# First conditioned norms, transposes and values of an attention block, for three of five tiles, made inside the block before it

## The reference, cut to what matters

```
# fourth layer: hidden = gelu(xn @ w1[e]); expert_out = hidden @ w2[e]; out = sum over e of gate * expert_out
x = x + L1_ffn(layernorm(x))
# fifth layer, on h = layernorm(x), four times:
y = ((h - mean) / sqrt(var + eps)) * (1 + scale) + bias     # scale = cond @ sw + sb, bias = cond @ bw + bb
q, k, v = y @ wq + bq, y @ wk + bk, y @ wv + bv             # 4 heads of 128
h = h + attention(q, k, v over the edges) @ wo + bo
y = (the same conditioned norm with second weights)
h = h + relu(y @ m_w1 + m_b1) @ m_w2 + m_b2
```

## Time and profile before

| what | value |
|---|---|
| median of 3 runs | 2746.47 us |
| profiled execution, own time | 2751.77 us |
| its span | 2750.0 us |
| PE busy | 2538.4 us, 92% |
| DVE busy | 1171.2 us, 43% |
| ACT busy | 758.4 us, 28% |
| POOL busy | 728.9 us, 27% |
| mean granted TensorE clock | 0.954 of full |

### The profile page before, as it was taken

The page is one execution under the profiler, slowest core; times in us unless marked ns, Lnnn a source line. Parts: engine busy times, 40 slices in busy tenths (PEclk is TensorE's granted clock), DMA queues, the critical chain, the costliest instruction groups (busy, mean ns, idle before and its releaser), DMA issues. The chain is left out here.

```text
span 2750.0 us, 33997 instructions
## 1 busy us (share of the span) xinstructions
PE 2538.4 (92%) x11318; PEld 1676.4 (61%) x11318; DVE 1171.2 (43%) x2661; ACT 758.4 (28%) x1487; POOL 728.9 (27%) x716
## 2 busy tenths in 40 slices
PE   4798969989989999899999999999999999789997
PEld 4465547757757655475665766666655665457774
DVE  8813965545535555353253433544222223530001
ACT  0521433323423322152251432521111121111121
POOL 0542855425425400001000010111444443101110
PEclk9898979999989998899999999999999999889998
DMA  3111036426326430111101102004999875548885
GB/s 83 43 54 62 12 106 185 119 81 195 111 78 198 112 128 12 42 47 51 55 16 37 54 21 77 1 19 139 285 281 276 231 217 154 112 160 315 315 288 175
DMA packets 91970, 340.22 MB, mean 124 GB/s; under 512 B 28896, under 2 KB 29024, under 8 KB 83618
## 3 DMA queue, kind: packets, MB, share of 16 engines
q1 hardware_dynamic: 51359, 245.90, 28.0%
q0 software_dynamic: 40448, 92.15, 11.8%
HBM read 338.60 MB, written 36.52 MB: 136 GB/s over the span
## 5 line engine op out<-in xcount | busy, mean ns | idle before, releaser
L84 PE MATMUL ps<-W,HT 128*128 128x320 f32 (+3 forms) x1432 | 534.4, 513 | 7.1 <-issue 3.5
L84 PEld LDWEIGHTS ps<-W,HT 128*128 128x128 f32 (+2 forms) x1432 | 256.6, 190 | 173.1 <-issue 120.8
L84 PE MATMUL ps<-XT,W 128*128 128x250 f32 (+1 forms) x1184 | 328.6, 433 | 3.1 <-ACT XT L1253 1.9
L84 PEld LDWEIGHTS ps<-XT,W 128*128 128x128 f32 x1184 | 225.5, 193 | 103.3 <-issue 20.5
L1031 PE MATMUL ps<-XN,W 128*128 128x512 f32 x504 | 264.7, 608 | 3.8 <-ACT GT L1304 2.6
L1639 POOL TENSOR_TENSOR H<-H,RB 125x512 f32<-125x512 f32 x40 | 50.7, 1267 | 737.2 <-DVE XN L1969 737.2
L2318 POOL DMA_INDIRECT result_rows<-KT,LOGC x110 | 112.6, 1024 | 466.1 <-DVE KT L2925 224.0
L84 PEld LDWEIGHTS ps<-HT,W 128*128 128x128 f32 x1152 | 133.8, 195 | 9.3 <-issue 8.1
L84 PE MATMUL ps<-HT,W 128*128 128x128 f32 x1152 | 134.0, 278 | 0.8 <-DVE HT L2915 0.8
L1007 POOL DMA_INDIRECT QT<-node_rows,LOGC x84 | 80.0, 952 | 205.2 <-DMA node_rows<-V 139.0
L1141 PEld LDWEIGHTS ps<-P,QT 128*128 128x128 f32 x672 | 91.7, 199 | 62.5 <-issue 62.5
(11 more groups left out here) (569 smaller groups left out, 4240.6 us busy)
## 6 DMA issues: line engine op xcount, KB each, us to landing
W<-in_L_ffn_w SPq DMA_DIRECT2D x38, 2048.0 KB, 7.4
W<-in_L_ffn_Wgu SPq DMA_DIRECT2D x92, 640.0 KB
W<-in_L_ffn_Wd SPq DMA_DIRECT2D x92, 320.0 KB
W<-in_L_gnn_Wqkv SPq DMA_DIRECT2D x4, 3072.0 KB, 10.3
W<-in_L_gnn_W SPq DMA_DIRECT2D x5, 2048.0 KB, 24.3
W<-in_L_gnn_Wm SPq DMA_DIRECT2D x4, 2048.0 KB, 7.7
W<-result_rows SPq DMA_DIRECT2D x5, 1344.0 KB
RB<-in_L_gnn_rows SPq DMA_DIRECT2D x24, 256.0 KB, 3.6
```

The lines of the kernel that those rows point to most:

```text
L84: last = nc.tensor.matmul(out, lhs(k), rhs(k), start=(k == 0), stop=(k == nk - 1))
```

## The change

Five things are moved from the head of `l2_gnn_block` into the tail of `l1_gnn_block`, for tiles 0 to 2 only (FIRST_TILES = 3): the conditioned norm, its two condition products, the transposes with their copy to XT, the value product and its bias add. The two `plus_one` go too. Each of the three tiles gets its own banks for its condition (0 and 1, 2 and 3, 6 and 7) and for transposes and value (1, 2, 3). DVE's list of the last expert is written out anew; the preparation of LOGC is moved one expert earlier (mask after x = 2, join after x = 3), and the logarithm on ACT with it (after x = 2). In `l2_gnn_block` PE starts with cond 3 and goes to the key columns; cond 4 stands after the second of them. Nine semaphores are made in the earlier block and live on. The arithmetic is the same.

```diff
             for x in range(NE):
+                if x == NE - 1:
+                    next_condition(0)
                 for t in range(T):
                     expert_row(x, t)
...
+            next_condition(1)
+            next_turned(0)
+            next_condition(2)
+            next_value(0)
+            for t in range(1, FIRST_TILES):
+                next_turned(t)
+                next_value(t)
...
+            def next_condition(t):
+                if t == 0:
+                    pe.wait_ge(g2["plus_one"], 1)
+                if t < 2:
+                    pe.wait_ge(s["e_out"], E_OUT[NE - 2 + t, 1])
+                else:
+                    pe.wait_ge(s["added"], T * (NE - 1) + 3)
...
+            def next_turned(t):
+                pe.wait_ge(g2["y_ready"], t + 1)
...
+            def next_value(t):
+                if t == 0:
+                    pe.wait_ge(p.g2_qkv, 16)
+                pe.wait_ge(g2["c_act"], t + 1)
...
-                if x == 3:
+                if x == 2:
                     act.wait_ge(s["cnt_max"], 1)
                     nc.scalar.activation(b.LOGC[0:R, :, :], b.P[0:R, :, :], ACT.Ln).then_inc(s["log_ready"], 1)
-            for t in range(T):
-                row_root("ovar", "ostd", b.std, b.mv, t)
+            for n in range(2):
+                act.wait_ge(p.g2_affine[n], 32)
+                nc.scalar.activation(b.affine[n][0:32, 0:D], b.affine[n][0:32, 0:D], ACT.Identity,
+                                     bias=b.ident[0:32, 16:17]).then_inc(g2["plus_one"], 1)
+            row_root("ovar", "ostd", b.std, b.mv, 0)
+            row_root("ovar", "ostd", b.std, b.mv, 1)
+            next_root(0)
+            next_turned_out(0)
+            row_root("ovar", "ostd", b.std, b.mv, 2)
+            for t in (1, 2):
+                next_root(t)
+                next_turned_out(t)
+            row_root("ovar", "ostd", b.std, b.mv, 3)
+            row_root("ovar", "ostd", b.std, b.mv, 4)
...
+            def next_norm(t):
+                dve.wait_ge(s["o_ready"], t + 1)
+                c.link(v.bn_stats(b.stats[0:R, t, :], b.H[0:R, t, :]))
+                v.bn_aggr(b.mv[0:R, t, :], b.stats[0:R, t, :]).then_inc(g2["var"], 1)
+                dve.wait_ge(g2["var"], t + 1)
+                dve.wait_ge(g2["cond_mm"], t + 1)
+                c.mark(v.scalar_tensor_tensor(b.XN[0:R, t, :], b.H[0:R, t, :], b.mv[0:R, t, 0:1],
+                                              b.ps[0:R, COND[t][0], :], ALU.subtract, ALU.mult))
+                dve.wait_ge(g2["std"], t + 1)
+                c.link(v.reciprocal(b.rstd[0:R, t:t + 1], b.std[0:R, t:t + 1]))
+                v.scalar_tensor_tensor(b.XN[0:R, t, :], b.XN[0:R, t, :], b.rstd[0:R, t:t + 1],
+                                       b.ps[0:R, COND[t][1], :], ALU.mult, ALU.add).then_inc(g2["y_ready"], 1)
...
-            output_normed(T - 1)
+            last_added(0)
+            last_added(1)
+            output_normed(0)
+            next_norm(0)
+            last_added(2)
+            output_normed(1)
+            next_norm(1)
+            output_normed(2)
+            next_norm(2)
+            last_added(3)
+            next_value_out(0)
+            last_added(4)
+            output_normed(3)
+            next_value_out(1)
+            output_normed(4)
+            next_value_out(2)
...
-            cond(0, 0, 0)
-            for t in range(3):
-                cond(0, 0, t + 1)
-                transposes(0, 0, t, 0, T1[t])
+            cond(0, 0, 3)
...
                 for m in range(NH):
                     columns(layer, KA + m, m, Wk, GA, s["k_mm"])
+                    if layer == 0 and m == 1:
+                        cond(0, 0, 4)
```

More of the change, by code:

```diff
@@ L867, in l0_ffn_block @@
     close_retired(retired)
+FIRST_NORM = ("plus_one", "cond_mm", "y_ready", "var", "std", "xt_mm", "v_mm", "v_out", "c_act")
+FIRST_TILES = 3
 def l1_gnn_block(nc, p, b, A, hb):
@@ L880, in l1_gnn_block @@
     p.g2_qkv, p.g2_wo, p.g2_wm, p.g2_cols_in = p.sems("g2_qkv_in", "g2_wo_in", "g2_wm_in", "g2_cols_in")
+    p.g2 = dict(zip(FIRST_NORM, p.sems(*(f"g2_{x}" for x in FIRST_NORM))))
+    g2 = p.g2
     p.g2_affine = p.sems("g2_affine_in0", "g2_affine_in1")
@@ L903, in l1_gnn_block @@
     FW2 = b.W[:, 11264:14336].rearrange("p (e n) -> p e n", e=NE)
+    WV = b.W[:, 4096:6144].rearrange("p (k n) -> p k n", k=KD)
+    COND = ((0, 1), (2, 3), (6, 7))
     GATING, SCALE = b.RB[:, 0:KD * NE], b.RB[:, 512:1024]
@@ L1105, in expert_row @@
                                  stop=True).then_inc(s["y_mm"], 1)
+            def next_condition(t):
[5 more added lines that the diff above has]
+                    pe.wait_ge(s["added"], T * (NE - 1) + 3)
+                for i in range(2):
+                    last = nc.tensor.matmul(b.ps[0:R, COND[t][i], :], b.GT[32 * i:32 * i + 32, t * R:(t + 1) * R],
+                                            b.affine[0][32 * i:32 * i + 32, i * D:(i + 1) * D], start=True, stop=True,
+                                            tile_position=(32 * i, 0))
+                last.then_inc(g2["cond_mm"], 1)
+            def next_turned(t):
+                pe.wait_ge(g2["y_ready"], t + 1)
+                for k in range(KD):
+                    last = nc.tensor.transpose(b.ps[:, 1 + t, k * R:(k + 1) * R], b.XN[0:R, t, k * 128:(k + 1) * 128],
+                                               b.ident[0:R, 0:R])
+                last.then_inc(g2["xt_mm"], 1)
+            def next_value(t):
+                if t == 0:
+                    pe.wait_ge(p.g2_qkv, 16)
+                pe.wait_ge(g2["c_act"], t + 1)
+                matmul_rows(nc, b.ps[0:R, 1 + t, :], lambda k: b.XT[:, k, t * R:(t + 1) * R], lambda k: WV[:, k, :], KD)\
+                    .then_inc(g2["v_mm"], 1)
             for u in range(GATHER_RING):
@@ L1236, in row_root, with next_root, next_turned_out @@
                     .then_inc(s[std], 1)
+            def next_root(t):
+                act.wait_ge(g2["var"], t + 1)
+                nc.scalar.activation(b.std[0:R, t:t + 1], b.mv[0:R, t, 1:2], ACT.Sqrt, bias=b.eps5[0:R, :])\
+                    .then_inc(g2["std"], 1)
+            def next_turned_out(t):
+                act.wait_ge(g2["xt_mm"], t + 1)
+                nc.scalar.activation(b.XT[:, :, t * R:(t + 1) * R],
+                                     b.ps[:, 1 + t, 0:KD * R].rearrange("p (k n) -> p k n", k=KD), ACT.Copy)\
+                    .then_inc(g2["c_act"], 1)
             def x_root(t):
@@ L1463, in output_normed, with last_added, next_value_out @@
                                 ALU.mult).then_inc(s["o_ready"], 1)
+            def last_added(t):
+                expert_added(NE - 1, t)
+                dve.wait_ge(s["added"], T * (NE - 1) + t + 1)
+                c.link(v.bn_stats(b.stats[0:R, t, :], b.X[0:R, t, :]))
+                v.bn_aggr(b.mv[0:R, t, :], b.stats[0:R, t, :]).then_inc(s["ovar"], 1)
+            def next_norm(t):
[10 more added lines that the diff above has]
+                                       b.ps[0:R, COND[t][1], :], ALU.mult, ALU.add).then_inc(g2["y_ready"], 1)
+            def next_value_out(t):
+                if t == 0:
+                    dve.wait_ge(p.g2_rows[0], 16)
+                dve.wait_ge(g2["v_mm"], t + 1)
+                v.tensor_tensor(b.V[0:R, t, :], b.ps[0:R, 1 + t, :], b.RB[0:R, 0:D], ALU.add).then_inc(g2["v_out"], 1)
             for t in range(T):
@@ L1534, in _ @@
             top_gate()
-            for x in range(NE):
+            for x in range(NE - 1):
                 for t in range(T):
                     expert_added(x, t)
[L1538 to L1543, removed]
                 if x == 0:
-                    for t in range(T):
+                    for t in range(T - 1):
                         c.mark(v.tensor_scalar(b.P[0:R, t, :], b.CNT[0:R, t, :], 1.0, None, ALU.max))
+                    c.wait()
+                    v.tensor_scalar(b.P[0:R, T - 1, :], b.CNT[0:R, T - 1, :], 1.0, None, ALU.max).then_inc(s["cnt_max"], 1)
                 if x == 1:
@@ L1550, in _ @@
                     c.wait()
-                    v.tensor_scalar(b.row_has[0:R, :], b.row_has[0:R, :], 1.0, None, ALU.min).then_inc(s["cnt_max"], 1)
-                if x == 3:
+                    c.mark(v.tensor_scalar(b.row_has[0:R, :], b.row_has[0:R, :], 1.0, None, ALU.min))
+                if x == 2:
                     dve.wait_ge(s["log_ready"], 1)
                     c.mark(v.tensor_scalar(b.P[0:R, :, :], b.CNT[0:R, :, :], 1.0, 1.0, ALU.min, ALU.subtract))
-                if x == 4:
+                if x == 3:
                     c.wait()
@@ L1566, in l2_gnn_block @@
     p.f2_in, p.f2_weights, p.f2_stored = p.sems("f2_in", "f2_weights_in", "f2_rows_stored")
-    s = semaphores(p, "g2", "chain", "plus_one", "cond_mm", "y_ready", "var", "std", "xt_mm", "v_mm", "v_out", "k_mm", "q_mm",
-                   "qb_mm", "qb_out", "c_act", "c_dve", "score_mm", "score_read", "shift", "exp", "p_ready", "pt_mm", "pt_out",
```

(16 more changed lines are left out.)

## The result

The changed kernel takes 2730.17 us (median of 5 runs, 2728.67 to 2734.81) against 2746.15 for the kernel before (median of 5, 2739.38 to 2748.47; three of them gave the 2746.47 that the forecast starts from): 16.0 us faster, ratio 0.9947 with a 95% interval of 0.9932 to 0.9963. The forecast was 2731.6, the range 2727 to 2738. The profiled execution took 2734.81, span 2733.1, so it is 16.9 us shorter in its span than the one before.

What follows compares the result with a forecast made beforehand. PE was taken to bound the kernel (busy 92%), with idle time and low clock in the tail. Key columns 16.0 us earlier, less 1.05 for condition 4, give 14.9 us: 2746.47 to 2731.6, range 2727 to 2738.

Steps and rivals of the forecast that it cites:

- LOGC for nothing, 2.1 us gained at the first add: DVE, last experts: earlier LOGC preparation costs nothing; expert 5's first add comes at 1091.35 against 1093.41.
- a table load before the Gelu of expert 3: ACT: a table load or a wait there was named as a sign that the forecast is wrong.
- `plus_one` nothing, condition 0 on the path with 1.05: Before expert 5's rows: both `plus_one` are done before PE asks; condition 0 on PE adds 1.05 us.
- Clock falls in the idle time: PE, tail: idle time of 2.3 us before tile 0's transposes drops the clock near 1098.4.
- rival (a): The clock stays up through the tail: 2.0 us more gained, 2729.6; chance 0.2.
- Back after 4 us: PE, tail: clock returns after 4 us of work, near 1102.7; value 0 runs from 1100.7 to 1105.15.
- DVE's wait for tile 2's root, off the path: Tail: root stands behind tile 1's copy on ACT, DVE waits 1.8 us; without that wait the sum stays 14.9.
- Boundary 0.39, no clock loss there: Start of next block: 0.39 us after DVE's last bias; PE's 1.2 us of idling there priced at nothing.
- Gain arrives whole: Key columns to the end: starting key columns earlier arrives whole at the end; that stretch unchanged within 2 us.

Runs made afterwards that it cites:

- unread products: Changed kernel plus two 512-column products nobody reads, in PE's idle time between condition 1 and tile 0's transposes: 2723.13 us against 2743.23, ratio 0.9928.
- tile 0 first: Changed kernel reordered: DVE normalises and conditions tile 0 before adding tile 1, ACT takes that root first, PE makes value 0 before condition 2: 2727.55 us, ratio 0.9945.
- LOGC late: Changed kernel with the preparation of LOGC put back one expert later (mask after x = 3, join after x = 4): 2733.51 us against 2743.23, ratio 0.9964.
- LOGC alone: Kernel before with only the preparation of LOGC (mask, join, logarithm) made one expert earlier: 2741.02 us against 2743.23, ratio 0.9990.

## Why the prediction was right

Shifted by the 2.76 us by which this execution is ahead at expert 4's rows, each step can be laid beside its forecast.

- *LOGC for nothing, 2.1 us gained at the first add.* The add stands at 1091.54 against 1091.35. The join left 0.99 us before expert 4's adds (forecast 1.0). Both LOGC experiments agree: 3.3 us alone, 2.6 lost when taken back. One sign that I had named for being wrong, a table load before the Gelu of expert 3, did appear (1061.39); it was badly chosen, since the load moves with the logarithm and still left 1.00 us to spare.
- *`plus_one` nothing, condition 0 on the path with 1.05.* PE waited for neither; placed between the rows, with shorter unread products, condition 0 gave back 0.93.
- *Clock falls in the idle time.* It fell, at 1098.0 against 1098.4 in forecast, and at the restart of PE or up to 0.2 us before it in all three traces of this tail's order. This was a choice among rows on either side, and their idle times are a weaker guide than I took them for (see the last section); rival (a), that it stays up, is what the unread products make true, for 3.1 us where I had 2.0.
- *Back after 4 us.* This term was mis-sized: the clock came back 6.7 us after PE's restart, between the two of the rows, which in windows of 0.1 us are 4.0 and 9.6 us and not the 3.8 and 9.4 that I read the earlier trace rows. Value 0 took 5.36 us (1098.36 to 1103.72) instead of 4.45, and the next block started 1.6 us late, at 1117.4: 0.4 us were lost before value 0, 0.9 in it and 0.3 behind it.
- *DVE's wait for tile 2's root, off the path.* 2.67 us instead of 1.8, for the same reason. Moving the root changed nothing in the tail. The copy and the root stand in ACT's trace in the order written, although the root's operand was made by 1101.70 and ACT idled 5.56 us before the copy. This agrees with the Trainium skill, page "TensorE: Matmul & The Clock Gate", section "Architectural detail: the array is 16× 32×32, not 1× 128×128", by which ScalarE is strictly first in, first out.
- *Boundary 0.39, no clock loss there.* The same 0.39, and PE's 1.12 us of idling left the clock at 1.00.
- *Gain arrives whole.* 697.54 and 698.65 us of attention.

Sum: 13.3 us in the tail against 14.9. The median moved by 16.0, and by 14 on the other chip (0.9948 of 2712.23); the intervals of either, 10 to 19 us, hold both 13.3 and 14.9. That the median lies 1.4 us from the forecast is thus partly luck: the tail is measured to a tenth of a microsecond, the total only to some 4 us.

What stays open: why the clock needed that long to return. The low level lasted 6.8 us in each of four traces: the three of this tail's order, where PE was busy nearly throughout, and that with tile 0 first, where it was busy for only the last 5.3 us. With LOGC late it lasted 10.2 us. No run varies the work in that stretch alone.

## What to carry to other kernels

Put dependent small work of the next stage beside a vector-bound tail together with enough wide products to fill the matrix engine: without the values the change shortens the tail by 5.4 us (47.86 to 42.42), 3.3 of them LOGC's, with them by 13.3. Then look at the first short idle time that is left; here 2.1 us of it cost 3.1 us more at the low clock, and two products that nobody reads bought them back. A wait at one engine is worth removing only if the last thing that the stage waits for comes earlier with it.

## What the runs showed that I had not expected

The length of an idle time did not decide whether the clock fell. With tile 0 first it fell after 0.99 us of idling, four transposes and another 0.3 us of idling; one of 1.12 us behind a full value left it at 1.00, and so did one of 1.49 us between two rows. PE had stood idle for 1.5 us when it fell with LOGC late, for 2.0 in the changed kernel, for 2.9 in the kernel before (at 1098.33), and for 4.6 with LOGC alone (at 1092.13).

And executions differ in stages far from the change: in the ten traces the routed experts take 404 to 413 us from the first to the last of their 320-column products. So a gain of 3 us, plain in the trace, was not to be told from nothing by eleven runs.
